# Edge counts of a graph layer: one PSUM sum per window of 16 targets instead of one copy and one addition per step

## The reference

```python
h0 = segment_sum(softmax_by_target(leaky_relu(el + er)) * feat[edge_type_8, src], dst)    # 8 relations, 4 heads
h1 = mlp(segment_sum(edge_nn[edge_type_2](x[src]), dst))                                   # 2 relations
h2 = sage(sage(x)), each with  msg_sum = segment_sum(xp[src], dst);  cnt = segment_sum(1, dst)
h3 = attention_of_first_edges(x)
```

## Time and profile before

| | |
|---|---|
| median of 3 runs | 1952.73 us (1949.06 to 1965.85) |
| span of the profiled execution, first to last instruction | 1946.7 us |
| instructions | 22362 |
| TensorE, VectorE, ScalarE, GpSimd busy | 75%, 59%, 40%, 27% of the span |
| mean granted TensorE clock | 0.752 |

### The profile page before, as it was taken

The page is one execution under the profiler, slowest core; times in us unless marked ns, Lnnn a source line. Parts: engine busy times, 40 slices in busy tenths (PEclk is TensorE's granted clock), DMA queues, the critical chain, the costliest instruction groups (busy, mean ns, idle before and its releaser), DMA issues.

```text
span 1946.7 us, 22362 instructions
## 1 busy us (share of the span) xinstructions
PE 1461.8 (75%) x5398; PEld 733.7 (38%) x5398; DVE 1153.3 (59%) x3024; ACT 786.8 (40%) x1243; POOL 531.3 (27%) x517
## 2 busy tenths in 40 slices
PE   5894765577666766666359999798999889989930
PEld 3342433231111111111237777554445444644620
DVE  5412432239888988898999999852181460450636
ACT  1331332237666766676200000035774527327121
POOL 0105555556757666775000000000000000000023
PEclk9996555575555555555559999899999989999975
DMA  3535455554545455554129888300000010000022
GB/s 149 166 141 170 143 164 166 173 162 142 177 150 177 150 166 170 173 172 151 44 84 307 270 271 269 96 1 24 1 1 1 0 33 1 1 11 1 1 61 63
DMA packets 84509, 223.94 MB, mean 115 GB/s; under 512 B 18456, under 2 KB 27588, under 8 KB 83908
## 3 DMA queue, kind: packets, MB, share of 16 engines
q1 hardware_dynamic: 60452, 158.01, 23.4%
q0 software_dynamic: 23968, 64.77, 12.6%
HBM read 140.09 MB, written 82.63 MB: 114 GB/s over the span
## 4 chain that ended last, share of the span: by engine, by line
PE 38%; DVE 15%; issue 6%; DVEq 2%; ACT 1%; DMA 1%; POOL 0%; another core or an unknown queue 0%; SPq 0%; POOLq 0%
PE bank L1750 15%; PE bank L1687 11%; PE bank L1770 2%; DVE arena L1126 2%; DVE arena L1084 2%; PE bank L1734 2%; DVE adjacency L1091 2%; PE bank L1709 1%; DVE arena L1085 1%; PE bank L1839 1%; PE bank L1836 1%; PE bank L1816 1%; DVE arena L1276 1%; DVE arena L1274 1%; DVE arena L1172 1%
## 5 line engine op out<-in xcount | busy, mean ns | idle before, releaser
L547 POOL DMA_INDIRECT arena<-feat_table,arena x469 | 494.5, 1054 | 365.6 <-issue 231.4
L1626 PE MATMUL bank<-arena 128*128 128x480 f16 x586 | 337.2, 577 | 165.9 <-DVE arena L1085 96.7
L629 ACT ACTIVATE arena<-bank 128x480 uint16<-128x480 f32 x586 | 332.6, 572 | 164.4 <-PE bank L1626 109.4
L1750 PE MATMUL bank<-arena 128*128 128x472 f16 x1440 | 291.4, 366 | 10.5 <-DVE arena L1276 6.5
L555 POOL DMA_INDIRECT arena<-al_table,edge_ends x15 | 14.3, 956 | 964.7 <-DMA al_table<-arena 960.4
L1091 DVE TENSOR_TENSOR adjacency<-adjacency,arena 128x480 uint16 x586 | 234.3, 400 | 38.8 <-issue 22.8
L1687 PE MATMUL bank<-arena 128*128 x966 | 229.5, 392 | 0.8 <-issue 0.3
L1626 PEld LDWEIGHTS bank<-arena 128*128 128x128 f16 x586 | 60.9, 104 | 442.4 <-issue 219.9
L1750 PEld LDWEIGHTS bank<-arena 128*128 128x128 bf16 x1440 | 141.8, 99 | 160.2 <-issue 12.4
L1085 DVE TENSOR_SCALAR arena<-iota,arena 128x480 f16<-128x480 f16 x586 | 199.0, 340 | 0.0
L1687 PEld LDWEIGHTS bank<-arena 128*128 128x128 f32 x966 | 174.0, 190 | 56.6 <-issue 35.3
(11 more groups left out here) (289 smaller groups left out, 1544.6 us busy)
## 6 DMA issues: line engine op xcount, KB each, us to landing
arena<-edge_rows SPq DMA_DIRECT2D x117, 520.0 KB, 4.7
edge_rows<-arena SPq DMA_DIRECT2D x67, 520.0 KB
edge_rows<-arena SPq DMA_DIRECT2D x67, 390.0 KB
feat_table<-arena SPq DMA_DIRECT2D x60, 260.0 KB, 2.1
arena<-feat_table,arena POOLq DMA_INDIRECT x469
arena<-in_w SPq DMA_DIRECT2D x1, 2048.0 KB, 10.1
arena<-in_xT SPq DMA_DIRECT2D x1, 1920.0 KB, 18.3
arena<-in_x SPq DMA_DIRECT2D x1, 1792.0 KB
```

The source lines that it names most:

```text
L547: g.indirect_dma_start(out=PLACE[k][:, t - lo, :], out_offset=None, in_=feat_t, in_offset=bass.IndirectOffsetOnAxis(ap=IE[:, t:t + 1], axi ...
L629: a.activation(EV[st % AS].rearrange("p r k -> p (r k)"), PS[4 + st % 4][:, 0:R2 * KW], ACT.Copy)\
L1626: mm(PS[4 + st % 4][:, 0:R2 * KW], OHS[st % AS], OHK[st % AS], start=True, stop=True).then_inc(s["a_mm"], 1)
L1750: ins = mm(PS[4 * fo + j][:, 0:CW], m[:, P * fo:P * (fo + 1)], ch[:, CW * j:CW * (j + 1)], start=(c == 0 and q == 0), stop=(c == n - 1 and ...
```

## The change

The counts of a window are added up in PSUM. TensorE's matmul no longer starts a sum but adds to what a bank holds. Window w uses the bank 4 + (w + 1) % 4. A table `CT` of 16-bit words holds for each step 512 * (window + 1); TensorE loads 8 words at a time into registers, takes the bank's column from the word's low bits, and waits until `a_free` has reached the word's high bits. ScalarE copies a bank straight into the window's place in `ADJ` when the last step of the window is done (it loads the 118 numbers of last steps, `ENDS`, 8 at a time, and waits on `a_mm` against them), then clears the bank of the window before, for the window three further on. The additions, the offsets and the clearing of the table are gone. VectorE's one-hot waits for the matmul of 8 steps before. `due` now counts windows. The ends come from a transpose of `cnt` that TensorE does in the first stage.

```diff
-            ZN = NW * SH * R2 // 2
...
-            def zero(lo, hi):
-                return a.activation(EARLY[:, lo:hi], ones[:, 0:1].to_broadcast([P, hi - lo]), ACT.Copy, scale=0.0)
+            def clear_bank(k):
+
+                a.activation(PS[4 + k][:, 0:R2 * KW], ones[:, 0:1].to_broadcast([P, R2 * KW]), ACT.Copy, scale=0.0)\
+                 .then_inc(s["a_free"], 1)
...
-            def a_evac(i, st):
-
-
-                act.wait_ge(s["a_mm"], i * AU + (st + 1))
-                a.activation(EV[st % AS].rearrange("p r k -> p (r k)"), PS[4 + st % 4][:, 0:R2 * KW], ACT.Copy)\
-                 .then_inc(s["a_ev"], 1)
-
-            for st in range(AS):
-                a_evac(0, st)
+
+            act.wait_ge(s["et_mm"], SC)
+            act.wait_ge(s["et_ev"], SC)
+            act.wait_ge(s["er_red"], NG)
+            for w in range(CBANKS):
+                clear_bank((w + 1) % CBANKS)
+            act.wait_ge(s["ends_ready"], 1)
             got = GC_ER + GC_ET
-            for n in range(A_N):
-                for u in range(AU):
-                    a_evac(n, AS + u)
-                    due = GC_ER + GC_ET + (NPB - 2 - GC_ER - GC_ET) * (AU * n + u + 1) // (A_N * AU)
-                    while got < due:
-                        collect(got)
-                        got += 1
-            for st in range(AS + A_N * AU, STEPS):
-                a_evac(0, st)
+            for w in range(WINS):
+                if w % CLOAD == 0:
+                    ends = nc.values_load_multi_w_load_instructions(
+                        ENDS[0:1, w:w + min(CLOAD, WINS - w)], engines=[ACTE], min_val=1, max_val=STEPS)[1]
+                act.wait_ge(s["a_mm"], ends[w % CLOAD])
+                a.activation(ADJ[:, :, KW * w:KW * (w + 1)],
+                             PS[4 + (w + 1) % CBANKS][:, 0:R2 * KW].rearrange("p (r k) -> p r k", r=R2), ACT.Copy).then_inc(s["a_ev"], 1)
+                if 1 <= w <= WINS - CBANKS:
+                    act.wait_ge(s["a_ev"], w)
+                    clear_bank(w % CBANKS)
+                due = GC_ER + GC_ET + (NPB - 2 - GC_ER - GC_ET) * (w + 1) // WINS
+                while got < due:
+                    collect(got)
+                    got += 1
...
+            dve.wait_ge(s["ends_mm"], 1)
+            v.tensor_copy(ENDS[0:1, 0:WINS], PS[4][0:1, 1:WINS + 1]).then_inc(s["ends_ready"], 1)
...
-            def add_step(i, st, off):
-                dve.wait_ge(s["a_ev"], i * AU + (st + 1))
-                dve.wait_ge(s["a_add"], i * AU + (st + 1))
-                dst = ADJ[:, :, bass.ds(off, KW)]
-                v.tensor_tensor(dst, dst, EV[st % AS], ALU.add).then_inc(s["a_add"], 1)
...
             with dve.Fori(0, A_N) as i:
-                offs = pair_offsets(i * (AU // 2), AU)
-
                 dve.wait_ge(s["a_oh"], i * AU + AS)
                 v.tensor_copy(SK, SLO_KEY[:, :, bass.ds(i * AU + AS, AU)]).then_inc(s["turn_cols"], 1)
                 dve.wait_ge(s["turn_cols"], i + 1)
                 for u in range(AU):
-                    add_step(i, u, offs[u])
+                    dve.wait_ge(s["a_mm"], i * AU + (u + 1))
                     onehots(AS + u, SK[:, 0, u:u + 1], SK[:, 1, u:u + 1])
...
-            def count(i, st):
+            pe.wait_ge(s["counts_table"], 1)
+            most = 512 * WINS
+
+            def count(i, st, word):
 
                 pe.wait_ge(s["a_oh"], i * AU + (st + 1))
-                if st >= 4:
-                    pe.wait_ge(s["a_ev"], i * AU + (st - 3))
-                mm(PS[4 + st % 4][:, 0:R2 * KW], OHS[st % AS], OHK[st % AS], start=True, stop=True).then_inc(s["a_mm"], 1)
-
+                pe.wait_ge(s["a_free"], word >> 9)
+                at = nc.s_assert_within(word & (512 * (CBANKS - 1)), 0, 512 * (CBANKS - 1), skip_runtime_bounds_check_because="a bank of the window's ring")
+                mm(CBANK[:, bass.ds(at, R2 * KW)], OHS[st % AS], OHK[st % AS], start=False, stop=False, skip_group_check=True)\
+                    .then_inc(s["a_mm"], 1)
```

64 lines of the change are left out of this document (24 added, 40 removed).

## The result

The changed kernel takes 2014.26 us (median of 4 runs, 2010.25 to 2034.32) against 1951.01 for the kernel before in the same series: a ratio of 1.032, 95% interval [1.027, 1.037]. It is 3% slower; the forecast was 1878 us. The profiled execution has a span of 2009.8 us, 63.1 more than before.

What follows compares the result with a forecast made beforehand. VectorE was taken to set the count stage's pace at 0.74 us a step, with GpSimd's gathers capping the gain. Scans ending at 876 instead of 951.8 us gave 1946.7 - 75 + 6 = 1878 us, range 1846 to 1938.

Steps and rivals of the forecast that it cites:

- TensorE's step: Count stage: a matmul step with register-picked bank was to take 0.42 us, so that VectorE still sets the pace.
- upper bound of 0.65: TensorE's count step with nothing overlapped: 0.40 us for the array plus 0.25 us of instruction work.
- nothing gained: Rival, chance 0.07: TensorE's count step at 0.70 us, or like waits at the collecting copies; about 1938 us.
- the rival at 0.60: Rival, chance 0.10: TensorE sets the count stage's pace at 0.60 us a step; 1904 us, up to 1913.
- The slower rival: Rival, chance 0.07: TensorE fetches code again at each loop turn, 14 us a turn in the count stage; 1983 us.
- VectorE's step: Count stage: two one-hots, 0.42 us, plus 0.05 for the loop's turn, 0.47 us a step.
- ScalarE's: Count stage: 586 bank copies become 118 copies and 118 clears, 335 us become some 130; ScalarE just keeps up.
- The gathers' pace: GpSimd in the count stage: 1.33 us a gather, between 1.23 and 1.40; 273 gathers take 363 us.
- The placement of the collecting copies: Copies even over 118 windows, 0.75 a window: GpSimd's first wait near 30 us instead of 9.8, then hardly any.
- The tail: From the last gather's end at 867 us to the scans' end at 876: 9 us, where 32.7 passed before.
- The later stages: All stages after the scans were to keep their lengths within 1 to 2 us.

Runs made afterwards that it cites:

- e6: Changed kernel with the gathers from part 43 on left out and their stores moved out of the count stage; count stage 401.3 us against 571.4.
- e3: Changed kernel with 16 steps in a loop's turn in place of 32; 2019.74 us, ratio 1.031 to the kernel before.
- e7: Changed kernel with 8 steps in a loop's turn in place of 32; 2030.64 us, ratio 1.041 to the kernel before.
- e1: Changed kernel with TensorE's 586 steps written out, bank and window wait as constants, no table loads or register arithmetic; 1915.45 us, ratio 0.977 to the kernel before.
- e8: e1 with the collecting copies placed by steps and ahead of the window's copy, as constants; 1910.66 us, ratio 0.982 to the kernel before.
- e2: Changed kernel with the collecting copies placed by steps and ahead of the window's copy, as constants; 2001.17 us, ratio 1.022 to the kernel before.
- e16: Changed kernel with bank offsets as unmasked 32-bit words and one wait for a free bank in four steps; 1940.48 us, ratio 0.991 to the kernel before.
- e9: Changed kernel with TensorE waiting for a free bank once in four steps, still by table and loop; 2001.11 us, ratio 1.004 to the kernel before.
- e4: Changed kernel with the table in 32-bit words and one more mask a step; 2024.31 us, ratio 1.034 to the kernel before.
- e12: Changed kernel with the gathers from part 43 on left out but the stores kept beside the count stage; count stage 443.9 us.
- e10: Changed kernel with as many gathers, but from part 43 on 16 bytes a row in place of 1040; count stage 582.1 us.
- e13: Changed kernel, gathers and stores left out of the count stage, GpSimd clearing a strip of its own three times per gather; count stage 401.5 us.

## Why the prediction was wrong

*The step that failed* is the second of the change: TensorE's step, "I take 0.42, near the lower end, since those 14 show the work going beside the array". With no disturbance at all it is 401.3 / 586 = 0.685 us (e6), above even the upper bound of 0.65. Two things were mis-sized. The instruction work was bounded with 0.25 us from the earlier trace rows, where a load brings four 32-bit words in 333 ns; here a load brings eight 16-bit words in 1.92 us, on a queue with six instructions a step that is as full as the array. And 0.40 for the array plus 0.25 for the queue was the wrong sum: the queue alone needs 0.41 to 0.43 for its six instructions and 0.24 for the load, one after the other, at either clock. Whether two costs hide each other is not asked of the later stage's rows but of the queue's instructions, counted.

*By the prediction's own working* a step of 0.70 us was the rival "nothing gained", 1938 us (0.07). (Worked out as for the rival at 0.60, with 33 windows and 283 steps bound by steps, the last gather would end at 914 and the time be 1925; the 1938 is 13 us too high.) The step was 0.69 and the time 2014, so that rival holds for the step and a second error of at least 76 us stands beside it: with gathers and stores beside it the stage is 170 us longer, most of it by the slow stretches. None of the rivals had them. The slower rival put the code fetch at each turn of the loop and got 1983; e3 and e7 show that the slow stretches do not come by turns, and that four times as many turns cost 1% at most (1.041 against 1.032). It looked at the right symptom, "two matmuls of 0.1 us in 1.4 us" in the earlier trace rows: this was a slow stretch of the kernel before, in the stage ahead, where gathers run as well. The argument against it, few instruction transfers in the records, held against a fetch at each turn, but it did not exclude slow stretches: 10 transfers are seen between 420 and 990 us in the changed kernel, beside some 20 of these. The Trainium skill, Runtime: NRT & Kernel Launch, "Instruction fetch mechanics", states that a taken branch out of the present two-page window forces a fetch. The loops of 8 and 16 steps do not agree with a cost by branches, and no run here shows whether such fetches are what is late.

*VectorE's step* was right: 0.47 forecast, 0.44 where nothing else holds it (e1, 113 steps in 50 us). *ScalarE's* was right: it waits 382.6 us for the matmuls. *The gathers' pace* was near: in the timeline between slow one-hots they come 1.25 us apart against the 1.33 taken; in e8, where one-hots run densely and additions are gone, (309.6 + 94.2) / 296 = 1.36 us. But they were never the bound in the changed kernel, since the steps were. *The placement of the collecting copies* made the first wait long, as forecast (41.6 us against the 30 named), but not "then hardly any": there were 42 of them, since the steps bound throughout. It cost 13 to 20 us (e2). *The tail* behind the last gather was to be 9 us; the last gather starts at 990.8 and the scans end at 1012.6, since the count ended last, at 994.4, as in the kernel before. *The later stages* kept their length: 63.1 us of span against 60.8 at the scans.

*The gain was real.* VectorE lost its additions and ScalarE four fifths of its copies (it got 118 clearings). What they gave up was put on TensorE's queue, which had 4 instructions a step and got 6 and a load, and this engine became the one that all wait for. e16 keeps the idea, takes nearly two instructions and two thirds of the loads' time away, and comes out 0.9% ahead of the kernel before.

## What to carry to other kernels

Count the queue instructions that a table-driven step adds to each engine, waits on registers and address computations too, and sum them in line with the register loads; on TensorE here 0.10 us for each register or address operation and 1.92 us for a load of eight 16-bit words. A matmul's array time hid the operations only where their sum was the shorter (e9 at half clock), and the load not even there. Put into the table what the instruction needs (the offset itself, in 32 bits, no mask or shift), and wait once for several steps where the order of the windows can't lock the kernel by it. Where gathers run beside a stage, an engine with many small instructions is the one that they slow down, so a bound taken with the gathers idle is not enough.

## What the runs showed of the hardware that was not expected

- Loads of eight words on TensorE's queue: 1.92 us from a 16-bit table, 0.59 us from a 32-bit one (e4). With stores running beside it the former is 2.73 us (e12).
- Slow stretches: with gathers of 128 rows running, register operations of 36 ns take 0.70 us or twice that, for 2 to 17 us at every 85 to 125 queue records (up to 46 us in e16), with rows of 16 bytes as with 1040 (e10), and never without gathers (e6, e12, e13).
- In e1 the granted clock was 0.93 from 450 to 500 us and VectorE was the limit; before it was 0.50 in every 50 us from 450 to 900 (for 600 to 650 us in the earlier trace rows), with steps of 0.74 us against the array's 0.40. In the changed kernel the queue's 0.41 and the array's 0.40 at half clock lie side by side.
- Two chips ran the kernel before in 1990 us instead of 1950. On one of them the changed kernel took 2028 instead of 2014, so its ratio is 1.018 there and 1.032 here.
